# A two-layer graph attention on one core: the V ring keeps sixteen slots longer, the split of W1 and the turned copies move, and VectorE takes over one sum of the last stage

## The reference

```python
enc = x
for l in range(2):
    q, k, v = ((x @ W[l] + b[l]).reshape(N, 8, 64) for W, b in (q, k, v))
    a = (q[dst] * k[src]).sum(-1) / 8
    e = exp(a - segment_max(a, dst)[dst])
    alpha = e / (segment_sum(e, dst)[dst] + 1e-16)
    x = segment_sum(alpha[:, :, None] * v[src], dst) + (x @ Ws[l] + bs[l]) + enc
x = layer_norm(x, ln_g, ln_b)
x = relu(x @ W1 + b1) @ W2 + b2 + x
x = layer_norm(x, ln_g, ln_b) + enc
out = layernorm(x_input + x)
```

## Time and profile before

| | |
|---|---|
| runs, median (lowest to highest) | 2162.43 us (2158.18 to 2165.14), 3 runs |
| profiled execution, its own time | 2160.31 us |
| its span from first to last instruction | 2158.5 us |
| TensorE / VectorE busy over the span | 1834.3 us (85%) / 1824.4 us (85%) |
| ScalarE / GpSimd busy over the span | 877.4 us (41%) / 1446.1 us (67%) |
| mean granted TensorE clock | 0.937 |
| second collection, first to last `weigh` | 1476.7 to 1882.9 us |
| last stage, first hidden matmul to the end | 1891.4 to 2158.5 us |

### The profile page before, as it was taken

How to read it: one execution, slowest core, us unless ns; L and a number is a source line. 1 busy time by engine, 2 the same in 40 slices (tenths; PEclk the granted TensorE clock), 3 DMA queues, 4 the chain that set the end, 5 groups by cost and what they waited for, 6 DMA issues and landing times. The chain is left out here.

```text
span 2158.5 us, 33515 instructions
## 1 busy us (share of the span) xinstructions
PE 1834.3 (85%) x7437; PEld 1392.7 (65%) x7438; DVE 1824.4 (85%) x2304; ACT 877.4 (41%) x2257; POOL 1446.1 (67%) x1417
## 2 busy tenths in 40 slices
PE   6778999998489999997889999957787878888987
PEld 5656666666267787875666666636566666676776
DVE  7659999999899998984999999998898999835554
ACT  3223333333365555552333333334666656532221
POOL 3067777777677777774777777776577777566553
PEclk9989999999699999998999999977999999998998
DMA  7588888888778888886888888886688888763321
GB/s 287 185 270 294 276 287 290 275 284 279 223 225 264 267 265 267 262 265 232 256 285 283 289 279 287 282 264 191 206 281 261 263 263 274 240 190 98 98 69 47
DMA packets 225518, 523.60 MB, mean 243 GB/s; under 512 B 39707, under 2 KB 81563, under 8 KB 225446
## 3 DMA queue, kind: packets, MB, share of 16 engines
q0 software_dynamic: 106624, 349.00, 51.7%
q1 hardware_dynamic: 115942, 168.54, 22.8%
q10 hardware_dynamic: 2880, 5.24, 0.7%
HBM read 446.94 MB, written 75.39 MB: 242 GB/s over the span
## 5 line engine op out<-in xcount | busy, mean ns | idle before, releaser
L850 POOL DMA_INDIRECT all_work<-k_rows,all_work x664 | 632.0, 952 | 217.6 <-issue 188.6
L850 POOL DMA_INDIRECT v_ring<-v_rows,coll_index x624 | 607.6, 974 | 224.5 <-issue 178.2
L1928 PE MATMUL coll_banks<-coll_ev,coll_hot 128*128 128x260 f32 x2656 | 651.3, 393 | 100.4 <-DVE all_work L2049 40.7
L1928 PEld LDWEIGHTS coll_banks<-coll_ev,coll_hot 128*128 128x128 f32 x2656 | 497.1, 193 | 228.6 <-issue 106.1
L1059 PE MATMUL score_q_ps<-score_q,score_hot 128*128 x1328 | 392.6, 420 | 89.2 <-DVE score_q L1099 56.1
L1087 DVE TENSOR_TENSOR all_work<-score_q_ps,all_work 128x1024 f32<-128x1024 f32 x332 | 404.6, 1220 | 38.7 <-PE score_q_ps L1059 20.1
L2035 DVE TENSOR_TENSOR coll_ev<-v_ring,coll_banks 128x1024 f32<-128x1024 f32 x328 | 397.9, 1214 | 11.3 <-DMA v_ring<-v_rows,coll_index 5.1
L1092 DVE TENSOR_REDUCE graph_edge<-all_work 128x1024 f32 (+1 forms) x332 | 397.8, 1209 | 0.0
L1059 PEld LDWEIGHTS score_q_ps<-score_q,score_hot 128*128 128x128 f32 x1328 | 255.6, 199 | 183.4 <-issue 132.7
L1166 ACT ACTIVATE score_hot<-score_local,all_iota_col 128x512 fp32r<-128x512 uint8 x166 | 120.0, 723 | 584.1 <-DVE all_work L1087 548.5
L2049 DVE TENSOR_TENSOR all_work<-all_work,coll_banks 128x520 f32 x354 | 244.5, 691 | 57.6 <-PE coll_banks L1928 46.5
(11 more groups left out here) (323 smaller groups left out, 2340.0 us busy)
## 6 DMA issues: line engine op xcount, KB each, us to landing
score_xt<-x_turned SPq DMA_DIRECT2D x42, 512.0 KB, 6.4
x_turned<-coll_xt SPq DMA_DIRECT2D x40, 512.0 KB, 4.4
all_work<-k_rows,all_work POOLq DMA_INDIRECT x664, 4.9
score_local<-local_dst SPq DMA_DIRECT2D x166, 64.0 KB, 6.5
x_turned<-keys_xt SPq DMA_DIRECT2D x20, 512.0 KB, 4.3
score_skip<-in_x SPq DMA_DIRECT2D x40, 256.0 KB, 4.9
v_rows<-score_v_out SPq DMA_DIRECT2D x40, 256.0 KB, 5.7
skip_rows<-score_skip SPq DMA_DIRECT2D x40, 256.0 KB, 3.8
```

The costliest lines, as they stand in the source:

```text
L850: nc.gpsimd.indirect_dma_start(rows(HALF * turn + s, first)[:, t, :], None, table, at).then_inc(arrived(HALF * turn + s, first), 16)
L1928: last = nc.tensor.matmul(sums[sum_slots[u]][:, part, :], m, ev[:, s % EVS, t, part * AGG // 2:(part + 1) * AGG // 2], start=s == 0 or t = ...
```

## The change

Five edits go together:

- **Ring.** The second layer's ring keeps sixteen slots until step 68 (`SWITCH`), eight after it. GpSimd's loop is written out three times (`UNROLLED`) instead of once, VectorE's and ScalarE's bodies 2 to 4 are written out as well.
- **W1.** All four raw quarters are loaded at the start, into the room of W2's raw copy; the four `weight_high` stand at steps 7, 9, 11 and 13 of body 4 and the four `weight_low` at steps 8, 10, 12 and 14. W2's load moves behind SyncE's loop, after half 15.
- **Turned copies.** ScalarE's `gain_and_shift` moves from step 3 to step 5 of a half and `high_part` from step 4 to step 6, behind `root`; VectorE's `low_part` moves from step 6 to step 7, behind `inverse_root`.
- **Order table.** VectorE's nine small instructions of `order_of_last_stage` move from before body 0 to after it.
- **Twice x.** `twice_enc` goes from GpSimd (two instructions) to VectorE (one), between lines 1398 and 1403 of a group's first pair.

```diff
         def twice_enc(g):                       # GpSimd's list
-            pool.wait_ge(enc_in, 16 * GB * (g + 1))
-            nc.gpsimd.tensor_tensor(enc, enc, enc, ALU.add).then_inc(enc_ready, 1)
-            pool.wait_ge(enc_ready, 2 * g + 1)
-            nc.gpsimd.tensor_tensor(enc, enc, across(shift), ALU.add).then_inc(enc_ready, 1)
...
+        def twice_enc(g):                       # VectorE's list
+            dve.wait_ge(enc_in, 16 * GB * (g + 1))
+            v.scalar_tensor_tensor(enc, enc, 2.0, shift.unsqueeze(1).to_broadcast([P, GB, C]), ALU.mult, ALU.add).then_inc(enc_ready, 1)
...
-            dve.wait_ge(enc_ready, 2 * (g + 1))
+            if pair[0] % GB == 0:
+                twice_enc(g)
+            dve.wait_ge(enc_ready, g + 1)
...
+        SWITCH = V_RING + HEAD + 3 * V_RING
+        def slot_of(n):
+            if n < V_RING:
+                return n
+            return (n - HEAD) % (V_RING if more or n < SWITCH else HALF)
...
+        def slot_before(n):
+            if n < V_RING + HEAD:
+                return -1
+            if n < 2 * V_RING + HEAD:
+                return n - V_RING - HEAD
+            return n - (V_RING if more or n < SWITCH + HALF else HALF)
...
                     sp.wait_ge(e_dve, QUARTS - BY_ACT)
-                    for i in range(2):
+                    for i in range(KC):
                         load_w1(i)
...
-                    sp.wait_ge(w_lo, KC)
-                    sp.dma_start(w2_raw[:], k.W2.rearrange("(c p) n -> p c n", p=P)).then_inc(w2_in, 16)
                     with sp.Fori(1, 4) as it:
                         for turn in range(4):
                             norms_in(4 * it + turn, turn, it)
+                    sp.wait_ge(w_lo, KC)
+                    sp.dma_start(w2_raw[:], k.W2.rearrange("(c p) n -> p c n", p=P)).then_inc(w2_in, 16)
...
-                        if weights and at in (2, 4):
+                        if more and weights and at in (2, 4):
                             weight_low(h, at // 2 - 1)
+                        if not more and weights and h == 1 and at % 2 == 0:
+                            weight_low(at // 4, at // 2 % 2)
...
-                        if lows[h] and at == 6:
-                            low_part(2 * it + h - (READY + 1), (h + READY + 1) % 2)
...
                             if not more and at == 7:
                                 inverse_root(j)
+                        if lows[h] and at == 7:
+                            low_part(2 * it + h - (READY + 1), (h + READY + 1) % 2)
...
-                        if not more and highs[h] and at == 3:
+                        if not more and highs[h] and at == 5:
                             gain_and_shift(half - (READY + 1))
                         if roots[h] and at == 6:
                             root(half - READY)
-                        if highs[h] and at == (0 if more else 4):
+                        if highs[h] and at == (0 if more else 6):
                             high_part(half - (READY + 1), (h + READY + 1) % 2, 16 * (it - 2 + h))
```

More of the change, by code:

```diff
@@ L826, in side_product, with gather_rows @@
     return nc.tensor.matmul(out, xt[:, a, c, :], w[b][:, c, :], start=c == 0 and n == 0, stop=False)
-def gather_rows(nc, k, pool, table, rows, sources, index, held, first_index, wait_index, asked, arrived, rows_used, used, steps, begun=0):
+def gather_rows(nc, k, pool, table, rows, sources, index, held, first_index, wait_index, asked, arrived, rows_used, used, steps,
+                begun=0, unrolled=0):
     n = HALF * TPS
@@ L841, in gather_half @@
         for s in range(n_steps):
-            count = used(half, turn, times, s)
+            count = used(turn, times, s)
             if not isinstance(count, int) or count > 0:
@@ L846, in gather_half @@
             pool.sem_inc(asked, 1)
-            first = isinstance(times, int) and times == 0
             for t in range(TPS):
                 at = bass.IndirectOffsetOnAxis(ap=index[:, turn, s * TPS + t:s * TPS + t + 1], axis=0)
[L850 to L855, removed]
+                nc.gpsimd.indirect_dma_start(rows(turn, times, s)[:, t, :], None, table, at).then_inc(arrived(turn, times, s), 16)
+    for times in range(unrolled):
+        for turn in range(begun if times == 0 else 0, turns):
+            gather_half(turns * times + turn, turn, times)
+    with pool.Fori(unrolled, halves // turns) as it:
         for turn in range(turns):
@@ L1696, in _, with gathered, weighed @@
             def _(pool):
-                def weighed(half, turn, times, s):
+                def gathered(turn, times, s):
+                    return (2 * V_RING * times if isinstance(times, int) else LATE) + HALF * turn + s
+                def weighed(turn, times, s):
                     n = HALF * turn + s
[L1701 to L1709, removed]
+                    if isinstance(times, int):
+                        before = slot_before(2 * V_RING * times + n)
+                        return 0 if before < 0 else weighed_by(before)
+                    return 2 * USES * times + weighed_by(slot_before(LATE + n) - LATE)
+                gather_rows(nc, k, pool, k.v_d, lambda turn, times, s: slot_rows(gathered(turn, times, s)), k.step_src[:], index, TURNS - 1,
+                            first_index, lambda half, turn, times: pool.wait_ge(index_in[turn], 16 * (times + 1)), asked,
+                            lambda turn, times, s: arrival(gathered(turn, times, s)), ev_dve, weighed, STEPS, 1, UNROLLED)
                 if not more:
@@ L2125, in _ @@
                 one_hot(1, 1)
-                if not more:
-                    order_of_last_stage()
                 dve.wait_ge(cleared, 1)
@@ L2260, in weight_high @@
                     else:
[L2261 to L2262 removed]
+                        act.wait_ge(ev_dve, weighed_by(SWITCH - 1))
+                        nc.scalar.activation(w1[0][:, 2 * m + i], w1_raw[:, 2 * m + i], ACT.Copy).then_inc(w_hi, 1)
                 def rows_up():
@@ L2325, in body @@
                                     take_e(1 - h, i, next_entries[i])
-                        if weights and at in (1, 3):
+                        if more and weights and at in (1, 3):
                             weight_high(h, at // 2)
+                        if not more and weights and s in (7, 9, 11, 13):
+                            weight_high((s - 7) // 4, (s - 7) // 2 % 2)
                         if more and weights and s == 5:
@@ L2352, in _ @@
                     act.wait_ge(columns_in, 16 * 3)
-                    body(1, (False, True), none, True, BODY, both)
-                    with act.Fori(2, LOOPS) as it:
+                    body(1, (False, True), none, False, BODY, both)
+                    for it in range(2, STEADY // BODY):
+                        body(it, both, none, it == STEADY // BODY - 1, BODY, both)
+                    with act.Fori(STEADY // BODY, LOOPS) as it:
                         body(it, both, none, False, BODY, both)
@@ L2358, in _ @@
                     stored = 16 * (BLOCKS // 2 - 1)
+                    high_part(j - 2, 1, stored - 16)
                     root(j - 1)
```

67 lines of the change are left out of this document (35 added, 32 removed).

## The result

The changed kernel takes **2145.0 us** (median of 4 runs, 2143.6 to 2145.9) beside 2161.5 for the kernel before (2158.2 to 2165.1), a ratio of 0.9923 with the interval 0.9905 to 0.994. Forecast were 2139 us, between 2126 and 2149. The profiled execution took 2145.88 us, its span is 2144.0, its mean granted clock 0.942. That is 14.4 us under the profiled execution of before.

What follows compares the result with a forecast made beforehand. VectorE was taken to pace the collection, TensorE with waits for ScalarE's pieces the last stage. Terms -17.5 - 5 - 2.5 + 1 + 0.8 = -23.2 us took the profiled 2160.31 to 2137.1, as median 2139 us, range 2126 to 2149.

Steps and rivals of the forecast that it cites:

- Twice x, the mechanism: Last stage: without its twice-x work GpSimd's sums start earlier, line 1398 shortens, TensorE's waits and low clock shrink; -17.5 us.
- rival A: Last stage: line 1398 is long for another reason than GpSimd's sums; +12 instead of -17.5, 2168 us, chance 0.04.
- Turned copies, -5: Collection, each half: earlier inverse_root shortens the 1.28 us stall, less a new stall at step 7; -5 us over 17 halves.
- Rival B: Collection: ScalarE has no room for the copies at steps 5 and 6; +32 instead of -5, 2176 us, chance 0.03.
- W1: Collection: weight pieces moved from body 1 to body 4; -2.5 us in body 1, +1 us in body 4.
- Ring and W2: Collection: longer ring gives 0 by itself, GpSimd ends some 9 us ahead; W2's load near 1760 us costs 0 (to +3).
- Order table: Around body 0: moving VectorE's small instructions wins 0.85 us in front and adds 1.63 us behind; +0.8 us.
- Rival C: Collection: GpSimd becomes the bound, last five bodies at 40.0 us instead of 38.4; +8, 2147 us, chance 0.08.

Runs made afterwards that it cites:

- h1: h0 with SyncE's store of the turned copies moved behind the loads of the next group's skipped rows; bodies 2 to 9 9.4 us shorter than h0's.
- h2: h0 with all three pieces of the turned copies back where the kernel before had them; 5.7 us under h0 from weigh to weigh, 1.2 by whole run.
- h0: Changed kernel with second-layer gathers of steps 32 to 159 narrowed to 256 of 512 columns (not the right ones); bodies 2 to 9 took 318.74 us.
- e3: Changed kernel with only ScalarE's pieces back at steps 3 and 4, low_part staying late; ratio 0.9931 to the kernel before, on a slow chip, inconclusive.
- e2: Changed kernel with only low_part back at step 6, ScalarE's pieces staying late; ratios to the kernel before 0.9938 and, on another slow chip, 0.9883.

## Why the prediction was right and where it failed

The time fell within the range, 6 us above the number. In the profiled execution, 8.8 us above its 2137.1, the collection took 11.2 us more than forecast (-5.7, measured +5.5) and the last stage 2.4 less (-17.5, measured -19.9). That the time is in the range is owed to the last stage and to the width of the range: the collection's sign was wrong.

- **Twice x, the mechanism: right.** From the first hidden matmul to the results' matmuls of group 1 the stage is 5.4 us shorter, forecast 5.2 (80.1 for 85.5 us). TensorE's wait there is 4.03, forecast 4.5 (2.40 in the trace of twice x alone). The three later groups give 15.2 us, forecast 13.5: the clock behind them came back in full, as the 1.00 of the window shows. The instruction takes 2.28 us, as the earlier trace rows had it. The tail costs 0.7, not 1.2. That line 1398 was long through GpSimd's sums is now seen from both sides, and rival A is out. By the Trainium skill's rule (SBUF - State Buffer, "Who interferes with whom") the trace agrees: 1.42 us alone, 3.48 beside two GpSimd low parts of 3.26 us.
- **Turned copies, -5: the step that failed.** It counted the vector and scalar instructions that move, and left out the transfer that `low_part` releases. Bodies 5 to 9 alone lost 8.6 us, outside the term's bounds of -15 and 0. The new stall of `add` at step 7 did come, 0.25 us forecast, 0.33 measured in the first halves of bodies 5 to 9 and less in the second. With the store out of the way (h1 against h2) the late pieces are worth some -4.1 us in bodies 2 to 9; the moved store costs 9.4 (h0 against h1). Both are sizes with narrowed gathers, from one trace each. With full ones the changed kernel shows the same rows, larger, and e3 against e2 that the loads follow the store, but what the store alone costs there no run shows.
- **Rival B** named the right sign and the wrong place: ScalarE had room for its copies. The price per half was 0.9 us against the kernel before (8.6 over ten halves), under the 1.1 from which B decides.
- **W1: right in the main.** Body 1 is 8.7 us shorter: 4.9 for the four `weight_low` and 3.8 more, forecast 2.5; its longest stall is 1.49 us for 3.73. Body 4 is 5.7 longer: 4.9 and 0.8, forecast +1, but its wait of `add`, 3.49 us, holds the store's price too, so W1's own share isn't separated. Bodies 2 and 3 are 1.9 longer together; the later ones lose 1.7 each.
- **Ring and W2: right.** GpSimd's one long stop (17.92 us, below) stands where it was expected, near step 76; its last gather starts 15.5 us before the last `weigh`, 9 forecast: the slower VectorE left it more. W2's load was issued at 1790.4, 30 us later than forecast, and bodies 7 and 8 (41.2 and 41.0 us) show nothing of it. **Order table**: the first `weigh` starts 1.3 us earlier and body 0 takes 0.6 more, forecast +0.8 in sum.
- **Rival C** did not come, since the bodies were at 41 us, not 38.4. In h1, at 38.0, it began in body 9.

Timeline of GpSimd in the changed kernel: the stop and the last gather; of VectorE, the last `weigh`.

```profile
1638.10 0.94 POOL L850 DMA_INDIRECT v_ring<-v_rows,coll_index  x1 [17.92 <-DVE coll_ev L2054]
...
1872.82 0.95 POOL L850 DMA_INDIRECT v_ring<-v_rows,coll_index  x1 [0.30 <-issue]
...
1888.31 1.21 DVE L2054 TENSOR_TENSOR coll_ev<-v_ring,coll_banks 128x1024 f32<-128x1024 f32 x1
```

## What to carry to other kernels

Whoever moves an instruction can move every transfer that waits for it. List those, and look at what runs on the other engines where they land: loads of registers first, since they stand on an engine's path and show only as idle time "for nothing". If such a load is in a loop with TensorE, its lengthening can be paid twice, the second time in the clock, as it was here. And a term of the sum that is many small gains, one per half, is worth one timeline of that half before it is believed; the store alone, placed later, is the version to try next on the changed kernel. Its gain is bounded: at GpSimd's 40.0 us a body the gathers lose their lead to bodies of 38 us, as h1's body 9 shows.

## What the runs showed of the hardware

- ScalarE's register loads in front of its first copy of entries in the second halves of the bodies (2 to 9) took 0.7 to 1.0 us in h1, with the 256 KB store ahead of them and the 512 KB one elsewhere, 1.3 to 1.8 in h0 with both some 3 to 4 us before the copy, and 1.7 to 2.3 in the changed kernel, with both and the full gathers. In the kernel before, with the full gathers and the 512 KB store 6 us before the copy, they took 1.2 to 1.4. That transfers lengthen these loads is what they show together; through which part of the memory was not measured.
- How steeply the clock answers: in h0 a wait of TensorE of 1.85 or 2.04 us in this loop left the next eight matmuls at 1.99 us, one of 2.15 put them at 2.94 and one of 2.21 at 3.59. In the changed kernel one of 2.62 us in body 4, at another place, left them at 1.99, and so did one of 2.26 in body 8 of e3.
- Three chips ran the kernel before in 2671 to 2696 us and two others in 2162 to 2165. Stops of VectorE before `add` that the trace lays to "remote", another core or an unknown queue, make 219 us in one profile of the former, of the some 500 us that a run takes longer there; ScalarE stops with it. The rest of the difference was not looked into.
